# One loop over 64 query blocks in place of two nested ones, on ScalarE alone, in a fused feed-forward, attention, feed-forward block

## What is computed

```python
x = x + 0.5 * ffn(layernorm(x), Wr, We)         # 8 experts, top 2, with a capacity
x = x + attention(layernorm(x), Wq, bq, Wk, bk, Wv, bv, Wo, bo)
x = x + 0.5 * ffn(layernorm(x), Wr, We)

# attention: 16 heads of 16 features, rotary q and k, q scaled by 16 ** -0.5
attn = softmax(einsum('bhsd,bhtd->bhst', q, k), axis=-1)
out = einsum('bhst,bhtd->bhsd', attn, v)        # then the output projection
```

## Time and profile before

| what | value |
|---|---|
| median of 3 runs | 6699.69 us (6685.01 to 6714.57) |
| profiled execution, its own time | 6703.76 us |
| its span in the trace | 6701.9 us |
| TensorE granted clock, mean of the span | 0.965 |
| first exponential of the attention | 947.56 us |
| last output copy of the attention | 6072.88 us |

### The profile page before, as it was taken

How to read it: one execution, slowest core, us unless ns; L and a number is a source line. 1 busy time by engine, 2 the same in 40 slices (tenths; PEclk the granted TensorE clock), 3 DMA queues, 4 the chain that set the end, 5 groups by cost and what they waited for, 6 DMA issues and landing times. The chain is left out here.

```text
span 6701.9 us, 158276 instructions
## 1 busy us (share of the span) xinstructions
PE 6309.1 (94%) x54288; PEld 2809.3 (42%) x54288; DVE 6035.4 (90%) x6991; ACT 4753.6 (71%) x8698; POOL 378.2 (6%) x604
## 2 busy tenths in 40 slices
PE   7888579999999999999999999999999999996888
PEld 5666423333333333333333333333333333333666
DVE  7888579999999999999999999999999999963666
ACT  2222128888888888888888888888888888883111
POOL 2222300000000000000000000000000000001221
PEclk9999759999999999999999999999999999998999
DMA  2222301010101001010101010101010100001110
GB/s 79 91 85 97 91 10 16 13 16 13 16 13 17 16 13 18 11 19 10 19 10 19 14 19 11 21 13 16 13 16 13 17 16 13 3 3 65 42 47 24
DMA packets 120648, 177.38 MB, mean 26 GB/s; under 512 B 61616, under 2 KB 78784, under 8 KB 116800
## 3 DMA queue, kind: packets, MB, share of 16 engines
q1 hardware_dynamic: 120128, 169.43, 10.9%
HBM read 100.17 MB, written 69.21 MB: 25 GB/s over the span
## 5 line engine op out<-in xcount | busy, mean ns | idle before, releaser
L975 DVE TENSOR_REDUCE at_mx<-at_m 128x1 f32<-128x1024 f32 x4096 | 5008.5, 1224 | 178.4 <-PE at_m L849 158.5
L948 ACT ACTIVATE at_ex<-at_s 128x512 f32<-128x512 f32 x8192 | 4448.8, 595 | 815.4 <-PE at_s L870 234.9
L849 PE MATMUL at_m<-at_k,at_q 48*128 48x512 f32 x8192 | 3026.9, 452 | 63.6 <-DVE at_mx L975 50.0
L870 PE MATMUL at_s<-at_q,at_k 50*128 50x512 f32 x8192 | 3020.2, 447 | 13.4 <-ACT at_ex L948 13.2
L880 PE MATMUL at_po<-at_ex,at_v 128*32 128x256 f32 x32816 | 2643.8, 394 | 31.7 <-POOL at_v L818 31.7
L849 PEld LDWEIGHTS at_m<-at_k,at_q 48*128 48x128 f32 x8192 | 1224.0, 188 | 1786.9 <-DVE at_mx L975 1666.6
L880 PEld LDWEIGHTS at_po<-at_ex,at_v 128*32 128x32 f32 x32816 | 648.5, 108 | 1529.8 <-issue 766.7
L870 PEld LDWEIGHTS at_s<-at_q,at_k 50*128 50x128 f32 x8192 | 1220.7, 186 | 63.1 <-ACT at_ex L948 62.4
L272 PE MATMUL fr_ps<-fr_weh,fr_xl 128*128 128x512 f32 x512 | 179.2, 433 | 118.1 <-DVE fr_acc L443 118.1
L824 POOL COPY at_v<-at_vst 128x1024 f32<-128x1024 f32 x16 | 16.7, 1043 | 4652.0 <-DMA at_vst<-v_by_head 4652.0
L1205 PE MATMUL bk_ps<-bk_weh,bk_xl 128*128 128x512 f32 x512 | 172.0, 418 | 65.8 <-DVE bk_acc L1331 65.7
(11 more groups left out here) (167 smaller groups left out, 2661.4 us busy)
## 6 DMA issues: line engine op xcount, KB each, us to landing
at_q<-q_parts SPq DMA_DIRECT2D x96, 256.0 KB, 4.8
at_k<-k_parts SPq DMA_DIRECT2D x96, 256.0 KB, 6.3
q_parts<-fr_parts SPq DMA_DIRECT2D x64, 256.0 KB, 2.2
k_parts<-fr_parts SPq DMA_DIRECT2D x64, 256.0 KB, 2.4
attended<-at_o SPq DMA_DIRECT2D x256, 34.0 KB
fr_x<-in_x SPq DMA_DIRECT2D x16, 512.0 KB, 4.3
after_ffn<-fr_acc SPq DMA_DIRECT2D x16, 512.0 KB, 3.0
v_by_head<-fr_v SPq DMA_DIRECT2D x16, 512.0 KB, 4.1
```

Source lines behind the costliest of these rows:

```text
L849: ins = pe.matmul(pm[w][:, h * QB:(h + 1) * QB], Q[p][rows, base + i * P:base + (i + 1) * P], K[p][rows, c * CW + h * QB:c * CW + (h + 1) ...
L870: pe.matmul(ps[event(t) % NS][:, :], K[p][rows, j * P:(j + 1) * P], Q[p][rows, sb_ * QU + g * QB:sb_ * QU + (g + 1) * QB], start=True, sto ...
L948: ac.activation(Ex[QUAD * (j % NX) + 2 * g + 1 - half][:, :], ps[event(t) % NS][:, :], ACT.Exp)\
L975: ve.tensor_reduce(out=mx[u][:, i, c:c + 1], in_=pm[w][:, :], op=ALU.max, axis=AX.X)\
```

## The change

ScalarE's function for a pair and its call through `pairs` go. In their place one loop of `NPAIR * SB` = 64 rounds runs over one unit, and the loop's counter is the unit's number. The instructions of a unit, their waits and what follows the last unit stay as they are. No other engine's code is edited.

```diff
@@ -950,11 +950,8 @@
                         if t == COPY_AT - 1:
                             take_output(u)
 
-                def step(r, k, n, more):
-                    with loop(nc, ac, 0, SB) as sb_:
-                        unit(k * SB + sb_)
-
-                pairs(ac, step)
+                with loop(nc, ac, 0, NPAIR * SB) as u:
+                    unit(u)
                 take_output(NPAIR * SB)
                 ac.wait_ge(s_e, NPAIR * SB * EVENTS + (E0 + 1))
                 ac.sem_inc(s_e, COPY_AT)
```

## The result

The changed kernel's median is 6639.17 us (5 runs, 6634.04 to 6641.29), that of the kernel before 6693.97 us (5 runs, 6685.01 to 6714.57). The ratio is 0.9907, with a 95% interval of 0.9882 to 0.9933: 0.93% faster. The profiled execution took 6634.04 us, its span is 6632.2 us, 69.7 us less than before.

The account below looks back on a forecast made before the run. VectorE's row maxima, 99.2% busy in the attention, were taken to set the pace. Gaps of 22.6 us plus 28.4 us of lower clock made 50.95, so 6703.76 - 50.95 = 6652.8 us; range 6638 to 6668, narrowly 6643 to 6663.

Parts of the forecast that it names:

- The place and the number of the gaps, and their removal: ScalarE's loops in the attention: 15 gaps at code-copy changes or starts, 18 long periods; removal wins 50.95 us.
- an inner loop's code thus stays with the engine; changing to another copy of the same code fetches it anew: ScalarE's attention loops: reason given for the gaps, from queue q14 showing no fetch in 280 us with three inner ways back.
- 63 ways back at nothing: ScalarE's new single loop: 63 added ways back cost nothing, as periods around the earlier inner ones were 79.00 us.
- the loop's code does not stay: Rival at ScalarE's 63 ways back: each pays for a fetch, 129 us (6782 us) to 339 us (6992 us); chance 0.05.
- the full gain: Attention: all 50.95 us won, 22.6 of gaps and 28.4 of lower clock, giving 6652.8 us; chance 0.84.
- The rule of the Trainium skill: ScalarE's loop: a body longer than two 16 KiB pages would pay at each of 63 ways back; set against the change.
- The price of a pause, its length less 0.45, and the lower clock behind some: Attention: a 2.5 us gap costs 2.05 us, 0.45 being absorbed; lower clock behind some gaps adds 28.4 us in all.
- The exit at nothing, and the back phase: Behind the last unit: the one remaining loop exit costs nothing, at most 3.69 us; back-phase ScalarE code only moves closer.
- the base of the sum: Whole kernel: 50.95 us taken from the profiled 6703.76, its 4.07 above the median not taken off; front and unit 0 unchanged.
- another engine's gap beneath: Rival at units 8 to 56: TensorE's own loop gap keeps 38.16 us, only 12.8 won, 6691 us; chance 0.07.
- the clock falling by itself: Rival in the attention: gaps go but clock drops of about 28 us have another source, 6681 us; chance 0.04.

Follow-up runs that it names:

- nest8: Changed kernel with two nested loops, 8 rounds of 8 units, around one copy of the unit's code: 6635.16 us, ratio 0.9902 to the kernel before.
- split4: Changed kernel's loop split into four single loops of 16 rounds, four copies of the unit's code, no nesting: 6640.79 us, ratio 0.9925 to the kernel before.
- no_hint: Changed kernel's loop without the hint at its back edge: 7045.50 us, ratio 1.0549 to the kernel before.
- two_units: Changed kernel with one loop of 32 rounds over two units, two code copies in the body: 6636.41 us, ratio 0.9917 to the kernel before.
- order_fill: Changed kernel, maximum matmuls ahead of unit 0 in the units' order, plus one unused matmul after each of the first 148: 6627.26 us, ratio 0.9888.
- The second profile of before: The kernel before, unchanged, in a second profiled execution: 6687.52 us median, ratio to itself 0.9987; unit 0 to unit 1 took 79.00 us.
- the second runs: Both kernels measured once more, unchanged: 6687.52 us for the kernel before (0.9987), 6637.38 us for the changed one (0.9901).
- pause_2048: Changed kernel plus one unused activation of 128 x 2048 ahead of each unit's first exponential: 6802.54 us, ratio 1.0152 to the kernel before.

## Why the prediction came out as it did

- **The place and the number of the gaps, and their removal**: right. The 18 long periods became 79.0 us, the stretch gave back 50.86 of the predicted 50.95 us, and the clock stays at 1.00. Nested loops or not, it is the change from one copy of the unit's code to another that made them (nest8, split4).
- **The reason, "an inner loop's code thus stays with the engine; changing to another copy of the same code fetches it anew"**: right as observed, and incomplete in two ways. The code stays only with the hinted way back (no_hint). And a fetch is not a gap: two_units fetches copy after copy without one. A gap appears where a hinted loop is left for code that is not there; that is what all the gaps of before and of split4 have in common, and neither nest8 nor two_units has both. What the fetch unit does inside was not seen; this is what fits all of the runs.
- **63 ways back at nothing**: right with the hint. The rival "the loop's code does not stay" is real without it: it was priced at up to 339 us over the full gain, and no_hint lost 342.25 us in the stretch. That the two agree is luck: each way back was to cost 2.05 us by its gap and 3.33 by the clock, and the shortest gaps cost 1.38, so the clock and longer gaps had more than their share. The rule of the Trainium skill, "Runtime: NRT & Kernel Launch", section "Instruction fetch mechanics", by which a taken branch out of the engine's window stalls for a fetch, is met by no_hint's way back in that it fetches and stalls; in the changed kernel, no such fetch appears. The prediction held the rule against the change because it took the body for longer than the window of two 16 KiB pages that it takes from the same section of the Trainium skill. At some 20 KB, the estimate from two_units, one copy fits into them and two copies do not, which agrees with what stayed (the changed kernel, nest8) and what was fetched anew (two_units). So the quiet inner loops were no evidence against the rule's size. What the size does not explain is no_hint, where a body that would fit is fetched at each pass.
- **The price of a pause, its length less 0.45, and the lower clock behind some**: right, measured again with a pause of another kind.
- **The exit at nothing, and the back phase**: right, 629.3 for 629.0 us.
- **The step that failed is the base of the sum.** It was written: "I don't take the 4.07 off, since the lost time from clock drops differs between executions, and the time without them should not", and before it "The first 947 us do not change, nor does the slow start of unit 0". The time without drops behind gaps does differ, by the place at which the clock rises in unit 0 and by the front phase: the two profiles of the kernel before, each less its own loss, give 6652.8 and 6637.9 us. From copy 0 to copy 1 the profiled execution took 92.70 us; ten of the eleven other profiles took 79.00 to 86.77, order_fill's 93.62. Taking its own start as given put 13.7 us of slow start into the forecast, of which a typical execution has about a third. The second profile of before, own time 6689.57, less its loss of 51.72 us, is 1.3 us from the changed kernel's median. A run of the kernel before beside two_units took 6662.10 us, which, less the 22.6 us that the gaps alone cost, is 6639.5: beside such a run the base of 6652.8 does not stand. As a difference the sum was good: 6693.97 - 6639.17 = 54.8 us against 50.95 predicted for the mechanism. What is left, about 4 us, lies inside the spread of the runs and was not taken apart (beside the second runs the difference was 6698.63 - 6637.38 = 61.3 us).
- **The two rivals of no gain** (another engine's gap beneath, the clock falling by itself) did not occur: no period between units 1 and 63 is over 79.05 us in the changed kernel.

## What to carry to other kernels

Look at the distance from one repeated instruction to the next over the whole run, not at the busy shares: 44 periods equal to within 0.02 us and 18 longer ones show where loops are left, at no cost in work. Keep one copy of a long loop body, or all copies in one plain loop (two_units is as fast), mark its way back, and don't leave such a loop for new code where the next engine waits on the first instruction. Subtract a mechanism's loss from a profiled execution only after its other stretches have been compared with a second profile; otherwise forecast the difference and take the runs' median as the base.

## What was not expected of the hardware

- A hint at a loop's back edge was worth 7045.50 - 6638 = 407 us here, 6% of the kernel: 342 from unit 1's copy to that of unit 63, through gaps of 1.80 to 2.22 us and a lower clock behind half of them, and 57 in the last unit, through the clock.
- Pauses of nearly one length differ in how often a lower clock follows. None does behind 1.3 us or less. It is 3 of 62 behind the pause of 1.68 us, 7 of 29 behind the gaps of 1.80 to 1.84 us in no_hint and 24 of 33 behind its gaps of 1.88 to 2.22 us, so up to there it becomes more frequent with the length. Behind the gaps of 2.4 us and more of the kernel before it is 4 of 8 in each of its two profiles, no more than that. What decides in a single case stays open.
- In order_fill TensorE was busy 19.75 of 20 us from 840 to 860 us, ahead of unit 0, and was granted 0.50; in unit 0, busy all the time from 932 to 974 us, its clock came back at 974. In the last units of pause_2048 and of no_hint, which have no maxima to compute, the clock fell and stayed low for 133.1 and 136.5 us, to within 1 us of the last copy, though TensorE was busy 120 of 120 us from 6040 to 6160 in pause_2048.
